# Mixture-of-experts first layer with high and low tokens side by side, and another order of two weight loads

## The reference, cut to what matters

```python
x = x + cross_attention(layernorm(x), ctx_1024, mask)      # 8 batches, 64 tokens each, 1601 keys
x = x + self_products(layernorm(x), W_q)
x = x + ffn(layernorm(x))

def ffn(x):                        # T = 512 tokens, d = 512, hidden 2048, 8 experts, 2 per token
    logits = xf @ gate_w + gate_b
    top_v, top_i = top_k(logits, 2);  top_w = softmax(top_v)
    for e in range(8):
        h = relu(xf @ w1[e] + b1[e])
        y = h @ w2[e] + b2[e]
        out = out + cw[:, e:e + 1] * y
```

## Time and profile before

| | |
|---|---|
| median of 3 runs | 1366.5 us (1365.25 to 1367.12) |
| profiled execution | 1364.21 us, span 1362.4 us |
| TensorE busy (matmul) | 1286.7 us, 94% of the span |
| VectorE busy | 806.8 us, 59% |
| ScalarE busy | 675.5 us, 50% |
| mean granted TensorE clock | 0.971 |
| the chain that ended last | 92% TensorE, 3% VectorE, 2% ScalarE, 1% DMA |

### The profile page before, as it was taken

The page is one execution under the profiler, slowest core; times in us unless marked ns, Lnnn a source line. Parts: engine busy times, 40 slices in busy tenths (PEclk is TensorE's granted clock), DMA queues, the critical chain, the costliest instruction groups (busy, mean ns, idle before and its releaser), DMA issues.

```text
span 1362.4 us, 23006 instructions
## 1 busy us (share of the span) xinstructions
PE 1286.7 (94%) x9009; PEld 1201.0 (88%) x9009; DVE 806.8 (59%) x2052; ACT 675.5 (50%) x1192; POOL 161.1 (12%) x87
## 2 busy tenths in 40 slices
PE   6999999999999999999999999977559999999996
PEld 6699999999999999999999999976548999988995
DVE  5356656666666566565665666657326566565664
ACT  5345445535544645544554553453134566666661
POOL 3003002201300400400310120010300000000030
PEclk9999999999999999999999999997669999999998
DMA  8002200300300220220220030040135666666652
GB/s 289 10 1 86 75 1 27 134 1 2 131 30 1 86 75 1 86 75 1 82 79 1 26 119 1 1 165 1 62 136 199 235 230 203 212 235 231 213 181 64
DMA packets 61429, 129.07 MB, mean 95 GB/s; under 512 B 3492, under 2 KB 21040, under 8 KB 61080
## 3 DMA queue, kind: packets, MB, share of 16 engines
q1 hardware_dynamic: 59160, 120.85, 25.8%
q0 software_dynamic: 2176, 6.95, 1.6%
HBM read 121.89 MB, written 15.34 MB: 101 GB/s over the span
## 4 chain that ended last, share of the span: by engine, by line
PE 92%; DVE 3%; ACT 2%; DMA 1%; issue 1%; POOL 1%; SPq 0%; DVEq 0%
PE work L792 34%; PE ptp L792 23%; PE pv L895 7%; PE ptp L882 6%; PE work L830 6%; PE ptp L1062 2%; PE ptp L1063 2%; PE ptp L1064 2%; PE ptp L1066 2%; PE ptp L1065 2%; PE work L799 1%; PE ptp L799 1%; DVE pt L1239 1%; ACT pt L541 1%; POOL x_rows L522 1%
## 5 line engine op out<-in xcount | busy, mean ns | idle before, releaser
L792 PE MATMUL ptp<-vw_hi,cx_hi 128*128 128x256 f32 x832 | 241.7, 291 | 0.0
L792 PE MATMUL ptp<-vw_lo,cx_hi 128*128 128x256 f32 x832 | 235.2, 283 | 0.0
L792 PE MATMUL ptp<-vw_hi,cx_lo 128*128 128x256 f32 x832 | 235.0, 282 | 0.0
L481 POOL TENSOR_TENSOR cx_lo<-raw,cx_hi 128x1664 fp32r<-128x1664 f32 x31 | 117.6, 3793 | 676.5 <-ACT cx_hi L541 676.5
L792 PE MATMUL work<-cx_hi,kw_hi 128*128 128x402 f32 x512 | 179.2, 350 | 10.2 <-DVE cx_lo L1176 8.5
L792 PE MATMUL work<-cx_lo,kw_hi 128*128 128x402 f32 x512 | 178.6, 349 | 0.0
L792 PE MATMUL work<-cx_hi,kw_lo 128*128 128x402 f32 x512 | 177.6, 347 | 0.0
L792 PEld LDWEIGHTS ptp<-vw_hi,cx_hi 128*128 128x128 f32 x832 | 158.9, 191 | 16.9 <-issue 16.9
L792 PE MATMUL work<-xg_hi,w_hi 128*128 128x192 f32 x512 | 142.1, 278 | 23.6 <-DVE xg_lo L1391 23.6
L1239 DVE TENSOR_TENSOR pt<-ptp,pt 128x512 fp32r<-128x512 f32 (+1 forms) x224 | 141.3, 649 | 34.7 <-ACT pt L541 31.2
L792 PEld LDWEIGHTS ptp<-vw_lo,cx_hi 128*128 128x128 f32 x832 | 159.1, 191 | 0.0
(11 more groups left out here) (217 smaller groups left out, 2495.1 us busy)
## 6 DMA issues: line engine op xcount, KB each, us to landing
w1raw<-in_w SPq DMA_DIRECT2D x32, 1024.0 KB, 5.2
w2raw<-in_w SPq DMA_DIRECT2D x32, 1024.0 KB, 6.0
raw<-in_ctxT SPq DMA_DIRECT2D x32, 832.0 KB, 5.8
pr<-in_mask SPq DMA_DIRECT2D x8, 800.5 KB, 4.4
xrow<-x_rows SPq DMA_DIRECT2D x7, 256.0 KB, 2.7
y_rows<-y_out_rows POOLq DMA_DIRECT2D x7, 256.0 KB, 2.4
kwraw<-in_kwT SPq DMA_DIRECT2D x2, 512.0 KB, 4.9
xin<-in_x SPq DMA_DIRECT2D x1, 1024.0 KB, 9.5
```

The costliest lines, as they stand in the source:

```text
L481: pool.tensor_tensor(cx[1][:, :, sl], raw[:, k % 2], cx[0][:, :, sl].bitcast(F32), ALU.subtract).then_inc(c_lo, 1)
L792: last = pe.matmul(dst, lhs(i, c), rhs(j, c), start=(c == 0 and (i, j) == (0, 0)), stop=(c == n - 1 and (i, j) == (1, 0)))
```

## The change

There are two edits.

**First layer.** `xg` becomes one tile in which, for each contraction step c, the high part (192 columns) and the low part (192 columns) stand side by side. Per block f and step c there are now two matmuls in place of three: w1's high part times all 384 columns, and w1's low part times the 192 high columns, added onto the first 192 of the result. So the bank of block f (now one of four, `work[f]`) holds the sum of two products in columns 0 to 191 and the third in columns 192 to 383. ScalarE reads the second half with the bias into `hf` (`low_part`), VectorE adds the first half (`summed_up`), ScalarE makes the high part with the ReLU (`hidden_hi`), and VectorE makes the low part with the ReLU (`hidden_lo`, now a SCALAR_TENSOR_TENSOR with `max` and `subtract`). TensorE waits for the sum of the block that had the same bank a piece before (`h_sum`, shown as `hidden_summed`), before each block. The transposed tokens move to `yb[2]` and `yb[3]` (`ptp2`, `pv`).

**Order of loads on SP.** At p = 1 the token rows come behind the w1 and w2 loads.

```diff
+            xg = sb(m, "xg", [P, C, 2, SLOTS], F32R)
...
             def expert(ph, e, fresh=False, last=False):      # SP
                 for p in range(NP):
-                    if p == 1 and not last:
-                        if fresh:
-                            sp.wait_ge(x_sent, 16 * 2 * TT)
-                        load_x(ph, e + 1)
                     if p < NP - 1:
                         load_w1(ph, e, p + 1, fresh and p == 0)
                     elif not last:
                         load_w1(ph, e + 1, 0)
                     load_w2(ph, e, p, fresh and p < 2)
+                    if p == 1 and not last:
+                        if fresh:
+                            sp.wait_ge(x_sent, 16 * 2 * TT)
+                        load_x(ph, e + 1)
...
+                def low_part(p, f):                            # ScalarE
+                    c = FC * (NP * n + p) + f
+                    act.wait_ge(h_full, c + 1)
+                    if not (fresh and p == 0):
+                        act.wait_ge(h_lo, c - 3)
+                    ...
+                    act.activation(hf[:, f], work[f][:, SLOTS:2 * SLOTS], ACT.Identity, bias=bias).then_inc(h_part, 1)
                 def hidden_hi(p, f):
-                    act.wait_ge(h_relu, FC * (NP * n + p) + f + 1)
+                    act.wait_ge(h_sum, FC * (NP * n + p) + f + 1)
                     ...
-                    act.activation(hs[:, p % 2, f, HI], hf[:, f], ACT.Copy).then_inc(h_hi, 1)
+                    act.activation(hs[:, p % 2, f, HI], hf[:, f], ACT.Relu).then_inc(h_hi, 1)
...
                 for f in range(FC):                            # TensorE, hidden(n, p)
-                    if f % 2 == 0 and not fresh:
-                        pe.wait_ge(h_relu, FC * (NP * n + p) + f - 2)
-                    last = products(work[f // 2][:, (f % 2) * SLOTS:(f % 2 + 1) * SLOTS],
-                             lambda i, c: w1s[i][:, s, c, f * P:(f + 1) * P],
-                             lambda i, c: xg[i][:, c])
-                    if f % 2:
-                        last.then_inc(h_full, 1)
+                    if not fresh:
+                        pe.wait_ge(h_sum, FC * (NP * n + p) + f - 3)
+                    for c in range(C):
+                        pe.matmul(work[f][:, 0:2 * SLOTS], w1s[0][:, s, c, f * P:(f + 1) * P],
+                                  xg[:, c].rearrange("p i n -> p (i n)"), start=c == 0, stop=False)
+                        last = pe.matmul(work[f][:, 0:SLOTS], w1s[1][:, s, c, f * P:(f + 1) * P], xg[:, c, 0],
+                                         start=False, stop=c == C - 1)
+                    last.then_inc(h_full, 1)
...
+                def summed_up(p, f):                           # VectorE
+                    dve.wait_ge(h_part, FC * (NP * n + p) + f + 1)
+                    dve.tensor_tensor(hf[:, f], work[f][:, 0:SLOTS], hf[:, f], ALU.add).then_inc(h_sum, 1)
+                def hidden_lo(p, f):
+                    dve.wait_ge(h_hi, FC * (NP * n + p) + f + 1)
+                    for lo, part in ((LO_MAIN, slice(0, P)), (LO_TAIL, slice(P, SLOTS))):
+                        ins = dve.scalar_tensor_tensor(out=hs[:, p % 2, f, lo], in0=hf[:, f, part], scalar=0.0,
+                                                       in1=hs[:, p % 2, f, part].bitcast(F32), op0=ALU.max,
+                                                       op1=ALU.subtract)
+                    ins.then_inc(h_lo, 1)
...
                     for f in range(FC):
-                        ...
+                        summed_up(p, f)
+                        if f:
+                            hidden_lo(p, f - 1)
+                    hidden_lo(p, FC - 1)
```

More of the change, by code:

```diff
@@ L41 @@
 FC = 4
-HB = FC // 2
 SLOTS = 192
@@ L275, in layer @@
             hs = sb(m, "h", [P, 2, FC, 2 * SLOTS], F32R)
-            xg = [sb(m, f"xg_{n}", [P, C, SLOTS], F32R) for n in ("hi", "lo")]
+            xg = sb(m, "xg", [P, C, 2, SLOTS], F32R)
             pick = sb(m, "pick", [P, TT, SLOTS], F32R)
@@ L709, in gathered @@
                     act.wait_ge(xg_full, 2 * n + i + 1)
-                    copy(xg[0][:, 2 * i:2 * i + 2], work[2 + i][:, 0:2 * SLOTS].rearrange("p (c n) -> p c n", c=2), xg_hi)
+                    copy(xg[:, 2 * i:2 * i + 2, 0], yb[2 + i][:, 0:2 * SLOTS].rearrange("p (c n) -> p c n", c=2), xg_hi)
             def outputs(ph, e):
@@ L732, in expert @@
                 n = e + E * ph
+                def low_part(p, f):
[3 more added lines that the diff above has]
+                        act.wait_ge(h_lo, c - 3)
+                    col = 16 * e + FC * p + f
+                    bias = b1T[:, col:col + 1] if isinstance(e, int) else b1T[:, bass.ds(col, 1)]
+                    act.activation(hf[:, f], work[f][:, SLOTS:2 * SLOTS], ACT.Identity, bias=bias).then_inc(h_part, 1)
                 def hidden_hi(p, f):
-                    act.wait_ge(h_relu, FC * (NP * n + p) + f + 1)
+                    act.wait_ge(h_sum, FC * (NP * n + p) + f + 1)
                     if f == 0 and not (fresh and p < 2):
                         act.wait_ge(p2_used, NP * n + p - 1)
-                    act.activation(hs[:, p % 2, f, HI], hf[:, f], ACT.Copy).then_inc(h_hi, 1)
+                    act.activation(hs[:, p % 2, f, HI], hf[:, f], ACT.Relu).then_inc(h_hi, 1)
                 for p in range(NP):
@@ L747, in expert @@
                     for f in range(FC):
-                        c = FC * (NP * n + p) + f
-                        if f % 2 == 0:
-                            act.wait_ge(h_full, HB * (NP * n + p) + f // 2 + 1)
-                        if not (fresh and p == 0):
-                            act.wait_ge(h_lo, c - 3)
-                        col = 16 * e + FC * p + f
-                        bias = b1T[:, col:col + 1] if isinstance(e, int) else b1T[:, bass.ds(col, 1)]
-                        act.activation(hf[:, f], work[f // 2][:, (f % 2) * SLOTS:(f % 2 + 1) * SLOTS],
-                                       ACT.Relu, bias=bias).then_inc(h_relu, 1)
+                        low_part(p, f)
                         if f:
@@ L995, in gather @@
                 for c in range(C):
-                    dst = work[2 + c // 2][:, (c % 2) * SLOTS:(c % 2 + 1) * SLOTS]
+                    dst = yb[2 + c // 2][:, (c % 2) * SLOTS:(c % 2 + 1) * SLOTS]
                     for t in range(TT):
@@ L1007, in turn_tokens @@
                 for c in range(C):
-                    dst, cols = work[2 + c // 2][:, (c % 2) * SLOTS:(c % 2 + 1) * SLOTS], slice(c * P, (c + 1) * P)
+                    dst, cols = yb[2 + c // 2][:, (c % 2) * SLOTS:(c % 2 + 1) * SLOTS], slice(c * P, (c + 1) * P)
                     pe.transpose(dst[:, 0:P], xrow[:, 0, cols], ident[:])
@@ L1088, in expert @@
                 for p in range(NP):
-                    if p == 2 and not last:
+                    if p == 2 and not ph and not last:
                         turn_tokens(n + 1)
@@ L1092, in expert @@
                         places(scattered(ph, e))
+                    if p == 3 and ph and not last:
+                        pe.wait_ge(put_done, ST * (scattered(ph, e) + 1))
+                        turn_tokens(n + 1)
                     if p < NP - 1:
@@ L1104, in experts @@
                 if ph:
+                    pe.wait_ge(y_out, TT * (scattered(ph, 0) + 1))
                     turn_tokens(E * ph)
@@ L1390, in gathered @@
                     dve.wait_ge(xg_hi, 2 * n + i + 1)
-                    dve.tensor_tensor(xg[1][:, 2 * i:2 * i + 2], work[2 + i][:, 0:2 * SLOTS].rearrange("p (c n) -> p c n", c=2),
-                                      xg[0][:, 2 * i:2 * i + 2].bitcast(F32), ALU.subtract).then_inc(xg_lo, 1)
+                    dve.tensor_tensor(xg[:, 2 * i:2 * i + 2, 1], yb[2 + i][:, 0:2 * SLOTS].rearrange("p (c n) -> p c n", c=2),
+                                      xg[:, 2 * i:2 * i + 2, 0].bitcast(F32), ALU.subtract).then_inc(xg_lo, 1)
             def row(e):
```

11 lines of the change are left out of this document (3 added, 8 removed).

## The result

| | before | now |
|---|---|---|
| median | 1365.9 us (4 runs, 1364.07 to 1367.12) | 1321.4 us (4 runs, 1320.06 to 1323.72) |
| profiled execution | 1364.21, span 1362.4 | 1321.02, span 1319.3 |
| TensorE, VectorE, ScalarE busy | 1286.7, 806.8, 675.5 us | 1261.8, 840.9, 675.8 us |
| mean granted clock | 0.971 | 0.979 |

The ratio is 0.9675, 95% interval 0.9659 to 0.9691: faster by 44.5 us. The forecast was 1321 us, in a range of 1309 to 1340. The total is hit to 0.4 us, but that is partly luck: the start of the experts gave about 4 us less than worked out, the experts themselves 3 us more, and 2 us came from an allowance that was not needed. The same kernel, run again later, gave medians of 1317.1 and 1321.6 us, so that a hit to 0.4 us is closer than the kernel itself repeats.

The account below looks back on a forecast made before the run. TensorE was taken to bound the experts, late loads their start, and afterwards the ScalarE-VectorE ring; 1364.2 less 45.8 (27.2 head, 15.4 experts, 3.2 last) gave 1318.4, with the median 2.3 above: 1321 us, range 1309 to 1340.

Parts of the forecast that it names:

- Edit 2, the wait that goes: Start of the experts: ScalarE's wait for w2 goes, hidden(0,0) starts at 981.1, 22.5 us earlier, behind the token selection.
- The new wait before hidden(0,1): TensorE in the head waits for VectorE's first sum behind its small steps: 2.97 us against 0.88, a new 2.1 us.
- The clock allowance: Low clock in the head: moves hidden(0,2) from 1004.8 to 1006.8; the forecast case allowed 0 to 5 us.
- the 12.1 us taken over from the kernel before: Head, before hidden(0,2): bias products, their additions and second(0,0), counted at 12.1 us from the old 12.07.
- A pair at 0.268: First layer on TensorE: a wide plus a narrow product costs 0.268 us (0.178 and 0.09), a block of 16 pairs 4.29.
- The ring: ScalarE and VectorE loop in each piece: 9.06 us, against 8.86 us that TensorE needs for it.
- the 0.06 for the operation: VectorE's new low part with maximum costs 0.06 us more than a plain one: 0.35 and 0.28 us.
- An expert's length: Distance between experts: 30.1 us of ring and next tokens, then blocks of 4.29 and 4.57: 38.96 us, gain 2.56.
- the wait of 1.8 us: Once an expert TensorE waits 1 to 2 us for the tokens' low part: 30.1 us against 28.3 alone.
- TensorE stays the bound: Rival, 10%: if a piece of the ring takes under 8.5 us, an expert takes 37.3 us and the total 1311 us.
- The sum: Whole kernel: head 27.2, six experts 15.4, last expert 3.2, together 45.8 us; output stays about 16 us.
- What I cost at nothing: Tokens in `yb[2]` and `yb[3]`, semaphores per block, later row loads: no cost; a late weight piece up to 7.9 us once.

Follow-up runs that it names:

- The loads alone: The kernel before with only SP's new order of loads, without the new first layer: 1339.5 us, ratio 0.9803.
- the first profile: Profiled execution of the changed kernel in the first comparison with the kernel before: 1321.02 us; median of those runs 1321.4 us.
- the repeat: The changed kernel run again without alteration, the first of two repeats: median 1317.1 us.
- The grouped products: The changed kernel with a block's four wide products first, then its four narrow ones: 1316.6 us in a single execution.
- the bf16 run: The changed kernel with the narrow product in bf16 on both sides and one more ScalarE copy an expert: 1327.3 us, ratio 0.9728.
- one more addition: The changed kernel with an extra unused 192-column VectorE addition in each piece, ahead of the first sum: 1322.2 us.
- the rearranged head: The changed kernel with place and weight transposes inside hidden(0,1) and VectorE's small steps behind piece 0's sums: 1315.4 us, later 1314.4 us.
- the layer alone: The changed kernel with SP's old order of loads, so only the new first layer: 1342.1 us, ratio 0.9831.

## Why the prediction was right, step by step

- **Edit 2, the wait that goes.** Right: 981.1 forecast, 981.15 measured, and the next thing that was late was the token selection, as said. The loads alone confirm it.
- **The new wait before hidden(0,1).** Right in kind and place, low by 1.4 us in the first profile (3.50 for 2.1), near in the repeat (2.20). **The clock allowance** of 2 us in the sum, for a stretch at a lower clock, was an estimate of mine that no run shows, and too small there: 13.7 us ran at a granted clock of 0.50 in the head, but about half of that, 6.8 us over the bias products and second(0,0), stood already in the 12.1 us taken over from the kernel before. What counts against the allowance is hidden(0,1), 7.64 us for 4.53: 3.1. In the repeat it was 1.8 (6.33), and the part behind took 1.3 less than the 12.1. Hidden(0,2) came at 1009.92, 3.1 later than forecast; in the repeat at 1005.98, 0.8 earlier.
- **A pair at 0.268.** Wrong: 0.285. The 0.09 of the earlier trace rows stood behind a 512-column product, and I read it as the price of the narrow one. It is only where one product's start falls; the price is that of the whole cycle. The upper bound from the old kernel's 0.111 a product was the better reading: a block of 16 pairs at 0.285 is 4.56, measured 4.53 to 4.64, against 4.29. The grouped products show 0.107 for a narrow one by itself. That the weight load is what a narrow product costs is not shown: the records of the float32 loads read 188 to 200 ns, and the straight line through 512 and 384 columns (0.228 and 0.178) would give 0.103 for 192 columns without it. In the bf16 run the load of the narrow product was recorded with 96 ns for 200, yet the block was not shorter (4.71 for 4.53).
- **The ring.** Right in shape, too long by 0.32 us a piece (9.06, measured 8.74). The low part with `max` costs 287 and 219 ns, what the plain one costs in the earlier trace rows (288), so the 0.06 for the operation, read from two instructions of 512 columns with different operands, was not there. A pair of low parts holds VectorE for 0.34 us (1133.37 to 1133.71 in the timeline) where I had 0.48, and two pairs stand in the path: 0.28 of the 0.32. The same price is most of why VectorE was busy 38.65 of 50 us for the 43 forecast: some 21 pairs fall into 50 us, 2.9 of the 4.4.
- **An expert's length.** Worked out 38.96, measured 38.44. The reason given, the ring and the tokens behind it, is the right one, but the wait of 1.8 us is not there: TensorE is held for about 0.1 us, in the weight load that opens an expert. From the end of second(2,3) (1116.10) to hidden(4,0) (1145.35) the path took 29.25 for the 30.1 forecast, mostly the 3 x 0.32 of the ring; the two blocks behind it took 9.19 for 8.86. TensorE by itself, one block of 4.64, three of 4.53, four second-layer blocks of 4.57 to 4.61 and 1.78 for the transposes, would need about 38.35. The rival "TensorE stays the bound" had 37.3 for it, with the wrong price of a pair. So the two errors, a ring too long and a pair too cheap, had opposite signs and met within 0.5 us: the mechanism was right, and that the length came out so near is partly luck.
- **The sum.** Head: 23 us at hidden(1,1) (1062.1 to 1039.2) for the 27.2 forecast. Six experts: 18.5 for 15.4. The last expert and the tail: the last copy of the output starts at 1302.59 instead of 1346.42, 43.8 earlier, so 2.4 are left for the last expert (3.2 forecast), and the output behind it took 0.7 longer, which is within what that stretch varies by (15.8 to 18.6 us in all profiles). (The granted clock is below full speed there too: the page of the kernel before shows it in its 28th to 30th and in its 40th slice.) Together 43.2 for 45.8; the median lay 0.3 above the profiled execution where I allowed 2.3, which hid the rest.
- **What I cost at nothing** stayed so: TensorE waits for no transfer between 1050 and 1250 us, and no engine is seen to wait for the buffers `yb[2]` and `yb[3]` to come free.

## What to carry to other kernels

When work moves from the busiest engine to others, write down the loop that the others form with their handovers and compare it with the busiest engine's period: here the two came out within 0.1 us of each other, with the loop the longer one, which no share of busy time shows (100% on TensorE, 77% and 70% on the others over 1050 to 1100 us). That no wait is recorded does not show that there is room: compare the distance between the end of what is needed and the start of what needs it with the same distance where a wait is certain, and look at whether the weight load still runs ahead. A price read from the distance of two starts belongs to the whole cycle of instructions, not to the one between them. And a load queued behind a wait that has nothing to do with it can cost as much as all the arithmetic of a change (27.0 us against 24.4 here): look at what stands behind each wait in a DMA issuer's queue.

## What the runs showed of the hardware

- A 192-column product with a fresh set of 128 weights cost 0.107 us in a row of its like (1132.85 to 1133.28 for four in the grouped run), a 384-column one 0.178 (1133.28 to 1133.99 for four); a wide and a narrow one in turn cost 0.285 in the changed kernel, the sum of both. In the kernel before a 192-column product cost 0.111 (5.34 us for 48).
- The first product behind a wait started 0.13 us after VectorE's end (990.16 to 990.29 at hidden(0,1) of the changed kernel, 1145.18 to 1145.31 at hidden(4,0) with one more addition). In hidden(4,0) of the changed kernel the weight load started with its product, and the first pair took 0.36 us; in hidden(4,1) the load started 0.22 us ahead, and the pair took 0.26.
- After a pause of 3.50, 2.20 and 3.34 us on TensorE (the three profiles of the changed kernel) the granted clock was 0.50 for 6.8, 3.4 and 3.4 us, most or all of it in hidden(0,1), which took 7.64, 6.33 and 6.21 us. A wide and a narrow product together took 0.53 us at that clock (990.91 to 991.44) for the 0.285 at 1.00. With no pause ahead (the rearranged head, twice) the block took 4.7 in its two halves. It was not so behind every pause: with the layer alone TensorE paused 2.20 us, and hidden(0,1) ran at full clock (1.00 over 1015.9 to 1020.5). In all these profiles another low stretch, of 3.4 or 6.8 us, began while the sparse bias products ran or within 2 us behind them.
- SCALAR_TENSOR_TENSOR took the time of TENSOR_TENSOR at 128 and 64 columns (287 and 219 ns). At 512 it took 747 for 686, with other operands.
- The changed kernel differed by 4.5 us between two chips (1317.1 and 1321.6) while the kernel before stayed within 2. Of the 6.8 us between the two profiled executions 2.3 lie before hidden(0,0), 2.3 between it and hidden(0,2), where the wait and the clock are, and 2.3 behind the last copy of the output. Whether it is the chip or the single execution that differs, these runs do not tell.
